# Gate and up projections as a two by two block product with seven products in place of eight

## The reference, cut to what matters

```python
mod = (silu(c) @ wmod).reshape(1, 6, 1, 512); sa, ca, ga, sb, cb, gb = ...   # rows of 512
ga, gb = clamped to at least 0.25 in size, sign kept
h = layernorm(x) * (1 + ca) + sa                     # x: 8192 tokens x 512
x = x + ga * linear_attention(h)                     # 16 heads of 32, causal
h = layernorm(x) * (1 + cb) + sb
gate = einsum('bsd,hd->bsh', h, w_gate / 127)        # w_*: int32 words, -127..127
up   = einsum('bsd,hd->bsh', h, w_up / 127)          # 512 -> 1536 hidden
x = x + gb * einsum('bsh,dh->bsd', silu(gate) * up, w_down / 127)
```

## Time and profile before

| what | value |
|---|---|
| three runs | 2197.57, 2194.55, 2196.25 us; median 2196.25 |
| the profiled execution | 2196.41 us, its span 2194.7 us, mean granted PE clock 0.996 |
| PE busy | 2138.8 us (97% of the span), 15216 instructions |
| DVE, ACT, POOL busy | 1260.3, 828.6, 830.2 us |
| attention, FFN | PE starts the FFN's first products at about 1097 us, ends at 2190 us |

### The profile page before, as it was taken

The page is one execution under the profiler, slowest core; times in us unless marked ns, Lnnn a source line. Parts: engine busy times, 40 slices in busy tenths (PEclk is TensorE's granted clock), DMA queues, the critical chain, the costliest instruction groups (busy, mean ns, idle before and its releaser), DMA issues. The chain is left out here.

```text
span 2194.7 us, 38965 instructions
## 1 busy us (share of the span) xinstructions
PE 2138.8 (97%) x15216; PEld 1745.3 (80%) x15216; DVE 1260.3 (57%) x1702; ACT 828.6 (38%) x1389; POOL 830.2 (38%) x630
## 2 busy tenths in 40 slices
PE   6999999999999999999899999999999999999999
PEld 4788887878878787888778888888888888888887
DVE  7998898898898898898633223332233322233211
ACT  5544444444445444445352123322233222333221
POOL 2643543443544433544433233333233332333333
PEclk9999999999999999999999999999999999999999
...
GB/s 244 38 51 49 73 45 59 73 59 59 73 45 59 74 59 59 69 48 50 149 125 39 39 38 11 29 38 38 38 10 29 38 38 38 14 24 38 39 20 20
DMA packets 61079, 117.38 MB, mean 53 GB/s; under 512 B 5137, under 2 KB 5137, under 8 KB 60946
## 3 DMA queue, kind: packets, MB, share of 16 engines
...
q10 hardware_dynamic: 528, 1.05, 0.1%
...
## 5 line engine op out<-in xcount | busy, mean ns | idle before, releaser
L1213 POOL TENSOR_TENSOR h_lo<-bv_row,h_hi 128x512 fp32r<-128x512 f32 x96 | 124.3, 1294 | 299.8 <-ACT h_hi L1271 299.8
L720 DVE RECIPROCAL r_den<-r_den 128x512 f32<-128x512 f32 x64 | 213.7, 3339 | 0.0
L387 POOL TENSOR_TENSOR x_res<-y,x_res 128x512 f32<-128x512 f32 x64 | 82.2, 1284 | 309.3 <-DVE y L743 309.3
L1213 POOL TENSOR_TENSOR h_lo<-k_sum,h_hi 128x512 fp32r<-128x512 f32 x96 | 124.0, 1292 | 189.4 <-ACT h_hi L1271 189.4
L1268 ACT ACTIVATE kv_diag<-pj 128x512 f32<-128x512 f32 x96 | 56.5, 588 | 343.3 <-PE pj L1389 343.3
L510 ACT ACTIVATE z_exp<-pj,qk_neg 128x512 f32<-128x512 f32 x128 | 88.1, 688 | 223.8 <-PE pj L956 196.9
L725 DVE TENSOR_TENSOR probs<-sc,causal 128x512 f32<-128x512 f32 x256 | 158.2, 678 | 2.4 <-PE sc L984 2.1
L956 PE MATMUL pj<-xt_hi,w_hi 128*128 128x512 f32 x512 | 151.1, 416 | 5.3 <-ACT xt_hi L502 3.5
L1350 DVE TENSOR_TENSOR k_sum<-pj,kv_diag 128x512 f32<-128x512 f32 x96 | 66.4, 692 | 155.6 <-PE pj L1389 113.8
L1271 ACT ACTIVATE h_hi<-bv_row 128x512 fp32r<-128x512 f32 x96 | 60.7, 632 | 247.7 <-DVE bv_row L1350 247.7
L1401 PE MATMUL num<-wd,h_hi 128*128 128x512 f32 x384 | 149.4, 389 | 0.0
...
## 6 DMA issues: line engine op xcount, KB each, us to landing
x_res<-in_L_attn_x SPq DMA_DIRECT2D x64, 256.0 KB, 2.9
x_mid<-x_res SPq DMA_DIRECT2D x64, 256.0 KB, 2.0
out<-y_rows SPq DMA_DIRECT2D x64, 256.0 KB, 2.0
xg<-in_L_attn_x SPq DMA_DIRECT2D x15, 1024.0 KB, 5.4
r_den<-in_ffn_words SPq DMA_DIRECT2D x36, 256.0 KB, 2.7
xg<-x_mid SPq DMA_DIRECT2D x9, 1024.0 KB, 5.5
r_den<-x_mid SPq DMA_DIRECT2D x8, 1024.0 KB, 5.6
wd_words<-in_ffn_words SPq DMA_DIRECT2D x12, 256.0 KB, 9.1
```

The lines of the kernel that those rows point to most:

```text
L387: pool.tensor_tensor(out=x_res[:, slot, :], in0=y[:, :], in1=x_res[:, slot, :], op=ALU.add).then_inc(y_ready, 1)
L720: dve.reciprocal(r_den[parity][:, c, :], r_den[parity][:, c, :]).then_inc(rden_ready, 1)
L1213: pool.tensor_tensor(out=h_lo[j], in0=h[j % 2], in1=h_hi[j].bitcast(F32), op=ALU.subtract).then_inc(h_lo_ready, 1)
```

## The change

Write the weight's two halves of 128 hidden units, gate and up, and the two halves of its 512 inputs as a block matrix A (A11, A12 gate; A21, A22 up), and the inputs of 1024 tokens as B with B11, B21 (the first 512 tokens, the two halves of the inputs) and B12, B22 (the second 512 tokens). A x B has four result blocks: gate of the first tokens, C11, gate of the second, C12, up of the first, C21, and of the second, C22. Plainly that is eight block products. The new kernel does the seven of the Winograd form of Strassen's algorithm:

- sums of weights: S1 = A21 + A22, S2 = S1 - A11, S3 = A11 - A21, S4 = A12 - S2, and of the inputs: T1 = B12 - B11, T2 = B22 - T1, T3 = B22 - B12, T4 = T2 - B21 (up to signs in the code)
- p1 = A11 B11, p2 = A12 B21, p3 = S4 B22, p4 = A22 T4, p5 = S1 T1, p6 = S2 T2, p7 = S3 T3
- C11 = p1 + p2; the rest from p1 + p6, p5, p7, p3, p4, partly by accumulation in the same bank, partly by ACT's copies (`save_p1`, `save_p5`, `save_u2`) and DVE's sums (`add_c11`, `add_c12`, `add_c22`).

What is written otherwise:

- **FFN groups** are of 1024 tokens, eight in all. Of each block q of 12, a product is 4 matmuls (two chunks, hi and lo): 7 x 4 = 28 in place of 2 x 16 = 32. `down` is done in two halves of six blocks, four banks in place of two; the first half's sum with x_mid is stored to x_mid and loaded again as the residual of the second half. A half's first four tiles come as five blocks, then the sixth (h of block 5 or 11 is the latest).
- **Weights**: in groups 2 to 13 of the attention the loop loads two blocks of gate and up and one of down, ACT makes them float (L614, L620), POOL makes the four sums for each of two chunks (eight 128x128 operations), SP stores the result to `parts` in memory. In the FFN SP loads 1 MB per q through a ring of four slots. `word_size` is taken twice at t = 1, once at t = 2, never at t = 3; the bound of the flag goes from 4096 to 1024. ACT waits at three `den_out` for transfers out of r_den (`down_out`, `made_out`).
- **Inputs**: x of a whole group is loaded by eight transfers of 256 KB, statistics wait for all. Turning comes in q = 8 to 11 (first four chunks, the first input half) and behind the last p4 (the other four). xf of both token halves go to four buffers; DVE makes T1 to T4 twice, ACT rounds seven operands twice, DVE makes five lo parts twice, POOL two (T3, T4).
- **First group**: its turning, sums and splits are put into the attention's last group.

```diff
+A11, A12, A22, A21, S2, S4, S1, S3 = range(8)
+B11, B21, T1, T4, T2, B22, T3 = range(7)
...
+        def store_made(g, parity, k):
+            wait(sp, unit_made, g * 8 + (4 * k - 12))
+            sp.dma_start(parts[bass.ds(g + (-2), 1), :, 4:8, k, :].rearrange("a p o n -> (a p) o n"),
+                         r_den[1 - parity][:, 2 + k, :].rearrange("p (o n) -> p o n", o=4)).then_inc(made_out[k], 16)
...
+            a11, a12, a22, a21 = (r_den[1 - parity][:, 2 + k, i * P:(i + 1) * P] for i in range(4))
+            pool.tensor_tensor(out=a22, in0=a21, in1=a22, op=ALU.add).then_inc(unit_made, 1)
+            pool.tensor_tensor(out=a21, in0=a11, in1=a21, op=ALU.subtract).then_inc(unit_made, 1)
+            wait(pool, unit_made, made + 1)
+            pool.tensor_tensor(out=a11, in0=a22, in1=a11, op=ALU.subtract).then_inc(unit_made, 1)
+            wait(pool, unit_made, made + 3)
+            pool.tensor_tensor(out=a12, in0=a12, in1=a11, op=ALU.subtract).then_inc(unit_made, 1)
...
             a_high(g * GT + 2)
+            if not isinstance(g, int):
+                unit_to_float(g, parity, 1)
             if two_ahead:
                 xt_full(g + 2, 1, x_bank)
...
-                act.wait_ge(most_ready, g * 3 - 2)
+                act.wait_ge(made_out[1], g * 16 + (-16))
             if ahead:
                 den_out(n, other, 3, den_bank)
...
-                word_size(g * 3 + (0 - 6), 0, parity)
+                word_size(g * 3 + (-6), 0, r_den[other][:, 2, :], (unit_in[0], g * 16 + (-16)))
+                word_size(g * 3 + (-5), 1, r_den[other][:, 1, :], (down_in, g * 16 + (-16)))
...
+            if not ahead and t >= 2:
+                pe.wait_ge(probs_ready, (tile + 1) * HPC)
+                turn_second(2 * t - 4, sc[:, 3, :])
...
+        def load_parts(G, q):
+            wait(sp, p4_ps, G * HB + (q - 3))
...
+        def h_low(G, q, i):
+            wait(pool, h_hi_ready, G * (2 * HB) + (2 * q + 2 - i))
+            b = q % 6 * 2 + i
+            pool.tensor_tensor(out=h_lo[b], in0=h[i], in1=h_hi[b].bitcast(F32), op=ALU.subtract).then_inc(h_lo_ready, 1)
...
+        def evacuate(G, i, bank):
...
+                wait(act, b_ready[B21], G * 2 + 1)
+                wait(act, sum_made, G * 8 + 4)
+            act.activation(xf[(0, 2, 1, 3)[which]], bank, ACT.Identity, bias=mod_col[:, SB, c:c + 1],
...
+        def step(G, q, extra):
+            save_p1(G, q)
+            save_p5(G, q)
+            silu1(G, q)
+            extra()
+            h_high(G, q - 1, 1)
+            save_u2(G, q)
+            h_high(G, q - 1, 0)
+            silu2(G, q)
...
+            in0, in1 = {T1: (b, a), T2: (d, full[T1][k]), T3: (d, b), T4: (c, full[T2][k])}[op]
+            dve.tensor_tensor(out=full[op][k], in0=in0, in1=in1, op=ALU.subtract).then_inc(sum_made, 1)
...
+        def low(G, op, k):
+            wait(dve, b_high, high_count(G, op, k))
+            dve.tensor_tensor(out=b_lo[op][k], in0=operand(G, op, k), in1=b_hi[op][k].bitcast(F32),
+                              op=ALU.subtract).then_inc(b_ready[op], 1)
...
+        def norm_stats(G, pair):
+            wait(dve, x_in, G * (16 * FT))
...
+        def step(G, q):
+            add_c22(G, q - 1)
+            add_c11(G, q)
+            times_gate2(G, q - 1)
+            times_gate1(G, q - 1)
+            add_c12(G, q)
...
+            sum_of(G + 1, T1, 0)
+            sum_of(G + 1, T2, 0)
+            add_c22(G, 11)
+            sum_of(G + 1, T3, 0)
+            times_gate2(G, 11)
+            low(G + 1, T1, 0)
+            times_gate1(G, 11)
+            sum_of(G + 1, T4, 0)
+            low(G + 1, T2, 0)
+            low(G + 1, B22, 0)
+            low(G + 1, B11, 0)
+            low(G + 1, B21, 0)
+            sum_of(G + 1, T1, 1)
+            gate_y(G, FT)
+            sum_of(G + 1, T2, 1)
+            sum_of(G + 1, T3, 1)
+            gate_y(G, FT + 1)
+            sum_of(G + 1, T4, 1)
+            gate_y(G, FT + 2)
+            low(G + 1, T1, 1)
+            gate_y(G, FT + 3)
+            low(G + 1, T2, 1)
+            low(G + 1, B22, 1)
+            gate_y(G, FT + 4)
+            low(G + 1, B11, 1)
+            low(G + 1, B21, 1)
+            gate_y(G, FT + 5)
+            gate_y(G, FT + 6)
+            add_c11(G + 1, 0)
+            gate_y(G, FT + 7)
...
+        def product(G, q, pairs, bank, start):
+            for op in {op: a for a, op in pairs}:
+                if q == 0:
+                    wait(pe, b_ready[op], G * 2 + 2)
+            passes = [(a, op, part, k) for a, op in pairs for part in (b_hi, b_lo) for k in range(2)]
+            for i, (a, op, part, k) in enumerate(passes):
+                mm = pe.matmul(bank, as_(blocks[q % 4][2 * a + k]), as_(part[op][k]), start=(start and i == 0),
+                               stop=(i == len(passes) - 1), skip_group_check=True)
+            return mm
...
+        def p6(G, q):
+            wait(pe, c11_ready, G * HB + (q + 1))
+            product(G, q, either([(S2, T2)], [(A11, T1), (A11, B11)]), xs[q % 2], not exact).then_inc(p6_ps, 1)
...
+        def p4(G, q):
+            wait(pe, c22_ready, G * HB + (q + 1))
+            product(G, q, either([(A22, T4)], [(A21, B11), (A22, B21)]), xs[q % 2], not exact).then_inc(p4_ps, 1)
...
+                    wait(pe, h_lo_ready, G * (2 * HB) + 2 * (half * 6 + j + 1))
...
+        def step(G, q):
+            p1(G, q)
+            p7(G, q - 1)
+            p2(G, q)
+            p5(G, q)
+            p4(G, q - 1)
+            p6(G, q)
+            p3(G, q)
...
+                for q in range(first + 1, first + 6):
+                    step(G, q)
+                    if ahead and q >= 8:
+                        wait(pe, y_gated, G * 16 + FT)
+                        turn(G + 1, q - 8, dn[q - 8])
+                i = half * FT
+                if half and ahead:
+                    wait(pe, xf_ready, G * 8 + 1)
+                down(G, i, range(5))
+                p7(G, first + 5)
+                if half and ahead:
+                    wait(pe, xf_ready, G * 8 + 2)
+                down(G, i + 1, range(5))
+                p4(G, first + 5)
+                if half and ahead:
+                    wait(pe, c11_ready, G * HB + HB)
+                    turn(G + 1, 4, sums[0])
+                    wait(pe, c12_ready, G * HB + HB)
+                    turn(G + 1, 5, sums[1])
+                    wait(pe, h1_ready, G * HB + (HB - 1))
+                    turn(G + 1, 6, xs[0])
+                    wait(pe, xf_ready, G * 8 + 4)
+                down(G, i + 2, range(5))
+                down(G, i + 3, range(5))
+                if half and ahead:
+                    wait(pe, xf_ready, G * 8 + 5)
+                    turn(G + 1, 7, sums[0])
+                for t in range(4):
+                    down(G, i + t, (5,))
+                for t in range(4, FT - 1):
+                    down(G, i + t, range(6))
+                if not half:
+                    p1(G, 6)
+                    p2(G, 6)
+                    p5(G, 6)
+                elif ahead:
+                    p1(G + 1, 0)
+                    p2(G + 1, 0)
+                    p5(G + 1, 0)
+                down(G, i + FT - 1, range(6))
```

879 lines of the change are left out of this document (568 added, 311 removed).

## The result

The changed kernel takes 2252.15 us (median of four runs, 2251.43 to 2254.09), the kernel before 2196.91 us (four runs). The ratio is 1.025, with a 95% interval of 1.0235 to 1.027: slower by 2.5%, where 2216 us and a range of 2150 to 2245 had been forecast. The profiled execution took 2252.76 us, its span is 2250.9 us.

A forecast was written before the change was run, and what follows sets the result against it. PE was taken to set the time in both stages. The terms -87.0 + 0 - 1.6 + 14.4 + 7 + 10.8 + 55 + 21 summed to +19.6 on 2196.4, forecasting 2216 us, range 2150 to 2245.

The forecast's parts named there:

- Matmuls: FFN: 384 fewer matmuls at 0.2267 us each, -87.0 us, the only gain.
- Steps: Inside an FFN block's step: the longest chain just fits under PE's 6.35 us, 0; +8 if 80 steps were 0.1 us late.
- Between the stages: Attention to FFN: old waits and half clock go, new waits of 10.8 us replace 12.4; -1.6 us, between -10 and +8.
- Attention: Twelve attention groups: second word_size and conversion delay PE's scores, +14.4 us; ACT waits for the sums' stores, +7.
- The store's wait: Attention group's end: ACT's den_out waits for the second unit's sums to be stored, 0.6 us a group, +7 us.
- Half ends: Nine FFN half ends: down's first tile waits 1.2 us for h_lo of the half's fifth block, +10.8 us.
- The boundary: Seven half ends preparing the next group: DVE's sums and lo parts slow beside POOL, 7.9 us each, +55; lower end 11.
- The next group's normalizing: FFN: normalizing beside POOL 9 us, evacuations and variance 5.6, statistics waiting for x loads 6; +21 us, low end 2.
- A (no alternation): FFN boundary: DVE and POOL do not alternate, part 7 costs 11 us and part 8 about 12; 2163 us, chance 0.25.
- B, the clock: FFN boundary: p1's and p2's waits lower the clock, 2.9 us more at each of seven; 2236 us, chance 0.10.
- C: Whole kernel: nearly all added work is covered, parts 4 to 8 leave 5 to 25 us; 2110 to 2135 us, chance 0.10.
- D: FFN: the flag picks the branch without sums, 40 float32 matmuls a block, far above 2300 us; chance 1 in 100.

The follow-up runs named there:

- f1: Changed kernel with e1 and e2 together, and group 1's x load issued in the attention's last group behind the down words' loads: 2196.1 us, ratio 1.0008.
- e2: Changed kernel, with the store of the second unit's four weight sums issued ahead of x_mid's store at t = 3: 2241.1 us, ratio 1.0207.
- f3: e1 with T3's and T4's lo parts made by DVE behind B21's, not by GpSimd (POOL): 2201.5 us, ratio 1.0025.
- f2: e1 with e4's order (B11 and B21 first) and the last turn in another PSUM bank, xs[1]: 2214.8 us, ratio 1.0089.
- e4: Changed kernel, with B11 and B21 rounded and their lo parts made first for the second half of the inputs: 2255.2 us, ratio 1.0274.
- e1: Changed kernel, with the next but one group's x loaded right behind the last turn, not behind the group's last store: 2217.3 us, ratio 1.010.
- e3: Changed kernel, with four blocks of down for each half's first four tiles, then block 4 for the four, then block 5: 2275.9 us, ratio 1.037.

## Why the prediction was wrong

The sign was right and the size was not: +19.6 us forecast, +56.2 by the two spans. Point by point:

1. **Matmuls, -87.0.** Right: PE has 384 fewer in the FFN, still 0.227 us each (2 in 0.455 us).
2. **Steps, 0, with +8 if each were 0.1 us late.** Right within some 7 us: the steps' small delays come to 1.6 us in a group of 1024 tokens, for 2.5 before, so some -7 in all eight. The chain that was to fit into a step was added up wrongly: 0.2 + 0.7 + 2 x 0.5 + 0.6 is 2.5 us, not 2.7. It fits into the step either way.
3. **Between the stages, -1.6.** Wrong in what it left out; by the account of the other parts it was about +13. Of the waits named, c11 cost 0.75 us and T3's lo parts 0.4, and 2.8 us went to T1's, which had not been named. Then PE waited 6.3 and 2.7 us for c22 in the first group:

```profile
1151.52 1.29 DVE L1588 BATCH_NORM_STATS2 stats<-xg 128x6 f32<-128x512 f32 x2 [6.71 <-DMA z_relu<-x_mid]
...
1159.07 1.78 DVE L1648 SCALAR_TENSOR_TENSOR r_den<-ga_row 128x512 f32<-128x512 f32 x1
...
1164.34 0.73 PE L1745 MATMUL sc<-w_hi,w_lo 128*128 128x512 f32 x2 [2.73 <-DVE bv_row L1622]
```

The first wait is for the load of group 1's x, priced at 2 us in the step; DVE stood 6.7 us for it, and PE ran at 1.2 GHz again. f1 gained 10 us there. The second is not for a load: ahead of that c22 DVE clamps gb, five operations from 1158.68 to 1162.4 (L1648 is the longest), and then takes statistics without a wait. No term had the clamp at this place, and f1 left this wait as it was. One reading was also off: after the two waits of the earlier trace rows the clock was at 1.2 GHz for 5.7 and 6.2 us of PE's work; the 2.8 us of the prediction are about what this cost.
4. and 5. **Attention, +21.4.** The sum was right, 22.4 measured. The shares were not. The store's wait, priced at 0.6 us a group between 0 and 1.6 (+7), cost 2.0 us in six groups and next to nothing in the other six; moving it gained 11 us (e2). The scores at t = 2 lost 0.6 of the 1.2 us forecast (0.94 against 0.33), 7 us for 14; the 3 to 4 us that are left are not told apart. I had the store landing in 2.0 us; it took 3.9 to 4.1 in the six groups and 2.3 to 2.5 in the others. The Trainium skill's rule on rows of 512 bytes ("DMA: Bandwidth & Descriptors", section "Specifications") was also read wrongly in the prediction: that such rows reach the full rate makes the store land as x_mid's does, in 2.0 us, and this gives the 0.6 us a group, not 0. Rows of 512 bytes are not shown as the cause of the 4 us: all these stores have them, and 2.3 us is their median on the page of the changed kernel. Nor is it the loads issued behind, since the loads of words and x follow within some 3 us in both kinds of group. Why every other one is slow stays open.
6. **Half ends, +10.8.** Right: 1.1 us at each of them, 1.3 with the restart.
7. **The boundary, +55.** Right in its mechanism and nearly in its size: 1.7 us at h_lo, 2.1 at the last turn, 0.7 to 1.6 at p1 and 0.6 at p2, with what follows each 7.6 us for 7.9. f3 shows the mechanism, f2 and e4 that reordering does not cure it.
8. **The next group's normalizing, +21, of it the load 1 us x 6.** This step failed. The prediction had the eight loads issued "behind the last turn". They are issued behind the group's last store, 23 us later, since SyncE takes its program in order. So the term was not 1 us but 4.3 in each of six groups, 2.7 of waiting and 1.6 from the lower clock: 26 us for 6. Moving the load gained 35 (e1), part of that by the side effect at the boundary. The other two terms of this step held: 2.3 us a group in small waits, 16 in all, for 14.6.

The miss is 36.6 us (56.2 less 19.6). The load in step 8 is 20 of them and step 3 some 15. Steps 3 and 8 share one mistake, apart from the clamp: a transfer's time was taken from when its buffer is free, not from what stands ahead of it on its queue. The rest is of both signs: the steps gave 7 us less, and the end of the program adds 3.5 us that no term had named: from PE's last matmul the span had 5.0 us before and has 8.5 now, because the residual of the last tiles is loaded into a ring of four behind the stores. These sizes are known to some 5 us, not to one.

**The rivals.** A (no alternation) is refuted by the 1.7 us operations in a row. B, the clock: it did fall, but not at p1, where B had put it. It fell at all six waits for c22 behind a late load and behind three of the seven waits at the last turn, for 3.4 us each time, so at about 1.7 us and not at the 2.9 of B. In e3, where p1 and p2 wait 1.5 and 0.6 us, it fell there too, in five groups of seven. C and D did not come.
